# A selective-scan layer behind three banded triangle layers: a third operand ring fed from DRAM, pairs of states multiplied at once, and stores moved behind loads

## The reference

```python
# layers 0, 1, 2, on xn = _ln(_gn(x)) * scale + bias
left = (xn @ Wl + bl) * mask * sigmoid(xn @ Wlg + blg)
right = (xn @ Wr + br) * mask * sigmoid(xn @ Wrg + brg)
out_gate = sigmoid(xn @ Wog + bog)
out = _banded_ingoing(left, right, 4)       # nine taps along one axis, 64 channels
out = _ln(out, out_norm_scale, out_norm_bias) * out_gate
return out @ Wo + bo

# layer 3, on _gn(x), for each of 256 columns over 256 time steps
xi, z = split(xs @ W_in)
xc = silu(causal_conv4(xi) + conv_b)
dt_r, Bc, Cc = split(xc @ W_x)              # 2, 16 and 16 wide
dt = softplus(dt_r @ W_dt + b_dt)           # 64 channels
h = exp(dt * A) * h + dt * B * x            # 64 channels x 16 states, step by step in time
y = einsum('bds,bs->bd', h, C) + xc * D_skip
return (y * silu(z)) @ W_out
```

## Time and profile before

| | |
|---|---|
| median of 3 runs | 2915.89 us (2911.53 to 2921.84) |
| the profiled execution | 2918.08 us, its span 2916.3 us |
| layer 0, 1, 2 of the triangle part | 30 to 404, 404 to 776, 776 to 1208 us |
| scan layer | set up from 1221 us, first scan 1254.4, last scan ends 2901.5 |
| busy over the span | PE 81%, DVE 80%, POOL 70%, ACT 64% |
| granted clock, mean | 0.94 of 2.4 GHz |

### The profile page before, as it was taken

The page is one execution under the profiler, slowest core; times in us unless marked ns, Lnnn a source line. Parts: engine busy times, 40 slices in busy tenths (PEclk is TensorE's granted clock), DMA queues, the critical chain, the costliest instruction groups (busy, mean ns, idle before and its releaser), DMA issues.

```text
span 2916.3 us, 37812 instructions
## 1 busy us (share of the span) xinstructions
PE 2360.2 (81%) x13018; PEld 741.1 (25%) x13018; DVE 2325.2 (80%) x2039; ACT 1853.9 (64%) x2534; POOL 2052.0 (70%) x1194
## 2 busy tenths in 40 slices
PE   4889878898888977478788887888878788787886
PEld 1233122441224421122222222222222222222221
DVE  5655566655565544389999999999999999999997
ACT  3624656245562434377778777777877778777773
POOL 2544244542445422269999999999999999999998
PEclk9999999999998988789999999999999999999997
DMA  4798316983159845676777767767777776767774
GB/s 162 244 328 247 106 45 211 342 275 108 52 183 343 276 136 149 134 178 169 185 176 180 188 166 187 177 175 183 174 188 172 184 178 177 189 165 188 177 176 113
DMA packets 257980, 538.30 MB, mean 185 GB/s; under 512 B 39624, under 2 KB 150992, under 8 KB 256896
## 3 DMA queue, kind: packets, MB, share of 16 engines
q1 hardware_dynamic: 230896, 469.09, 59.2%
q0 software_dynamic: 19040, 64.24, 7.5%
q10 hardware_dynamic: 7856, 2.56, 0.4%
HBM read 396.46 MB, written 139.33 MB: 184 GB/s over the span
## 4 chain that ended last, share of the span: by engine, by line
DVE 24%; issue 16%; ACT 9%; PE 7%; POOL 1%; DMA 0%; ACTq 0%; DVEq 0%; SPq 0%; POOLq 0%
DVE m_hs L473 13%; DVE m_pb L468 12%; ACT m_da L410 4%; PE m_pb L304 2%; ACT L366 1%; ACT m_act L358 1%; ACT L352 1%; PE m_py L284 1%; PE m_misc L242 1%; PE m_py L277 1%; ACT m_act L364 1%; POOL m_hs L486 1%; DMA m_dtb<-dt_rows 0%; PE m_misc L234 0%; PE m_misc L265 0%
## 5 line engine op out<-in xcount | busy, mean ns | idle before, releaser
L486 POOL TENSOR_TENSOR m_hs<-m_hs,m_cs 128x1024 f32<-128x1024 f32 x512 | 1200.4, 2359 | 130.2 <-DVE m_hs L473 80.2
L473 DVE TENSOR_TENSOR_SCAN m_hs<-m_da,m_pb 128x1024 f32<-128x1024 f32 x416 | 951.3, 2287 | 19.1 <-ACT m_da L410 4.7
L304 PE MATMUL m_pb<-m_dtx,late 64*128 64x512 f32 x1664 | 502.3, 677 | 233.7 <-DVE m_hs L473 226.2
L468 DVE TENSOR_TENSOR m_pb<-m_pb,m_bs 128x1024 f32<-128x1024 f32 x416 | 502.8, 1209 | 9.2 <-PE m_pb L304 9.0
L410 ACT ACTIVATE m_da<-m_dtb,m_a_neg 128x1020 f32<-128x1020 f32 x416 | 466.5, 1143 | 3.5 <-DMA m_dtb<-dt_rows 1.3
L1484 POOL TENSOR_TENSOR t_xc<-t_xc,big 128x512 f32<-128x512 f32 x96 | 120.2, 1270 | 333.2 <-DVE big L1390 333.0
L304 PEld LDWEIGHTS m_pb<-m_dtx,late 64*128 64x128 f32 x1664 | 155.3, 200 | 555.6 <-DVE m_hs L473 320.1
L284 PE MATMUL m_py<-m_hs,late 128*32 128x512 f32 x2048 | 277.0, 613 | 7.3 <-POOL m_hs L486 7.3
L1362 DVE SCALAR_TENSOR_TENSOR t_xc<-t_bank,t_vec,t_xc 128x512 f32<-128x512 f32 x96 | 72.0, 750 | 244.2 <-PE t_bank L1052 244.2
L1247 ACT ACTIVATE t_sq<-t_bank 128x512 f32<-128x512 f32 x192 | 106.9, 598 | 227.3 <-PE t_bank L1091 227.1
L1481 POOL TENSOR_TENSOR t_sq<-big 128x512 f32<-128x512 f32 x96 | 102.9, 1082 | 186.2 <-ACT big L1229 109.2
(11 more groups left out here) (160 smaller groups left out, 3847.0 us busy)
## 6 DMA issues: line engine op xcount, KB each, us to landing
m_dtb<-dt_rows SPq DMA_DIRECT2D x512, 512.0 KB, 5.7
late<-right_factor POOLq DMA_DIRECT2D x102, 512.0 KB, 6.2
right_factor<-t_tile SPq DMA_DIRECT2D x192, 256.0 KB, 3.9
t_tile<-band_out SPq DMA_DIRECT2D x183, 256.0 KB, 4.1
band_out<-t_vwin SPq DMA_DIRECT2D x48, 512.0 KB
band_out<-t_vwin SPq DMA_DIRECT2D x48, 480.0 KB
dt_rows<-m_dt SPq DMA_DIRECT2D x64, 256.0 KB, 4.6
t_xc<-in_x_cm SPq DMA_DIRECT2D x4, 2048.0 KB, 14.5
```

The costliest lines, as they stand in the source:

```text
L304: m = nc.tensor.matmul(pb[s % 2][:, half(n)], spread[rows, dg, :], dtx[par][rows, half(q)], start=True, stop=True)
L468: nc.vector.tensor_tensor(products, products, bs[q][:, :], ALU.mult).then_inc(u_done, 1)
L473: nc.vector.tensor_tensor_scan(hs[:, g % H_RING, :], decays, products, 0.0, ALU.mult, ALU.add).then_inc(h_ready, 1)
L486: nc.gpsimd.tensor_tensor(hs[:, g % H_RING, :], hs[:, g % H_RING, :], cs[q][:, :], ALU.mult).then_inc(hc_ready, 1)
```

## The change

Scan layer. `POOL_U` differs by the parity of the chunk: three products in even chunks (steps 5, 10, 15), four in odd ones (4, 8, 12, 15), 16 more in all. dt*x for these products no longer comes by TensorE and ScalarE: SyncE stores both halves of `dtx` to DRAM in step 2 of the same chunk and reads eight rows back, each to 16 partitions, into `ub`, now a ring of three. GpSimd's multiply by C runs in odd steps alone, over two slots of `hs` at once. Triangle layers. bc3 is a step later in the plan and stands near the front of it, behind the gate projection on TensorE and at the front of the part that waits for matmuls on VectorE. SyncE loads unit 14 two steps earlier than it did and unit 15 one step; the gates of unit 0 are opened ahead of its squares.

```diff
-    POOL_U = (5, 10, 15)
-    UB_RING = 2
+    POOL_U = ((5, 10, 15), (4, 8, 12, 15))
+    UB_RING = 3
...
-        USE = {op: i for i, op in enumerate(("u5", "bq1", "cq1", "u10", "x", "z", "dt", "u15", "bq0", "cq0"))}
-        OWN_USE = ("u5", "bq1", "cq1", "u10", "u15")
+        USE = {op: i for i, op in enumerate(("bq1", "cq1", "x", "z", "dt", "bq0", "cq0"))}
+        OWN_USE = ("bq1", "cq1")
...
+        def pool_step(j):
+            kk, i = divmod(j, PER_TWO)
+            par = int(i >= len(POOL_U[0]))
+            return S * (2 * kk + par) + POOL_U[par][i - len(POOL_U[0]) * par]
...
             "gpsimd": {1: [(OWN, "u5")], 3: [(POST, "gate1")], 6: [(OWN, "u10")], 9: [(PRE, "dtx0")], 10: [(PRE, "dtx1")], 11: [(OWN, "u15")],
                        13: [(OWN, "gate0")]},
-            "sync": {14: [(POST, "store")], 15: [(PRE, "dt_rows")]},
-        }
+            "sync": {2: [(OWN, "dtx_rows")], 4: [(OWN, "u5")], 6: [(OWN, "u10")], 8: [(OWN, "u15")], 14: [(POST, "store")], 15: [(PRE, "dt_rows")]},
+        }, {
+            "gpsimd": {1: [(OWN, "u4")], 3: [(POST, "gate1")], 5: [(OWN, "u8")], 8: [(OWN, "u12")], 9: [(PRE, "dtx0")], 10: [(PRE, "dtx1")], 11: [(OWN, "u15")],
+                       13: [(OWN, "gate0")]},
+            "sync": {2: [(OWN, "dtx_rows")], 4: [(OWN, "u4")], 5: [(OWN, "u8")], 7: [(OWN, "u12")], 11: [(OWN, "u15")], 14: [(POST, "store")], 15: [(PRE, "dt_rows")]},
+        })
...
+                    if s % 2 == 0:
+                        return
                     g_.wait_ge(h_ready, g + 1)
-                    nc.gpsimd.tensor_tensor(hs[:, g % H_RING, :], hs[:, g % H_RING, :], cs[q][:, :],
-                                            ALU.mult).then_inc(hc_ready, 1)
+                    two = hs[:, (g - 1) % H_RING:(g - 1) % H_RING + 2, :]
+                    nc.gpsimd.tensor_tensor(two, two, cs[q][:, :].unsqueeze(1).to_broadcast([P, 2, W]), ALU.mult).then_inc(hc_ready, 2)
...
                         j, q = pool_products(k, int(op[1:])), int(op[1:]) // DG
+                        g_.wait_ge(ub_loaded[j % UB_RING], 16 * (j // UB_RING + 1))
                         for n in range(2):
-                            g_.wait_ge(misc_used[n], use(k, op) + 1)
+                            g_.wait_ge(misc_used[n], use(k, f"bq{q}") + 1)
                         nc.gpsimd.tensor_tensor(ub[j % UB_RING][:, :], ub[j % UB_RING][:, :], bs[q][:, :], ALU.mult).then_inc(ub_ready, 1)
                         return
                     q = int(op[3])
                     g_.wait_ge(misc_used[q], use(k, "dt") + 1)
+                    if not early(k, 2):
+                        g_.wait_ge(dtx_stored[par], stores_of(k - 2, par))
                     nc.gpsimd.tensor_tensor(dtx[par][:, half(q)], dt[:, half(q)], act[par][:, half(q)], ALU.mult).then_inc(dtx_ready, 1)
...
+                def load_u(k, par, s):
+                    j = pool_products(k, s)
+                    q, i = divmod(s, DG)
+                    sp.wait_ge(dtx_stored[par], stores_of(k, par))
+                    if j >= UB_RING:
+                        sp.wait_ge(h_ready, pool_step(j - UB_RING) + 1)
+                    rows = dtx_dram[par, q, DG * DGS[i]:DG * DGS[i] + DG, :, :].rearrange("d n c -> d (n c)")
+                    sp.dma_start(ub[j % UB_RING][:, :],
+                                 bass.AP(rows.tensor, rows.offset, [[0, P // DG], [W, DG], [1, W]])
+                                 ).then_inc(ub_loaded[j % UB_RING], 16)
...
+                    if op == "dtx_rows":
+                        sp.wait_ge(dtx_ready, 2 * k + 2)
+                        if not early(k, 2):
+                            sp.wait_ge(ub_ready, pool_products(k - 1, 0))
+                        for n in range(2):
+                            sp.dma_start(dtx_dram[par, :, :, n, :].rearrange("q d c -> d q c"),
+                                         dtx[par][D * n:D * n + D, :].rearrange("d (q c) -> d q c", q=2)).then_inc(dtx_stored[par], 16)
+                        return
...
                 for n in blk[::2]:
-                    steps[at]["bc3"] += [n, n + 1]
+                    steps[at + 1]["bc3"] += [n, n + 1]
                     at += 2 if at < 69 else 1
...
+        LOADS = [[] for _ in STEPS]
+        for n in A3:
+            LOADS[A3_STEP[n] - {14: 3, 15: 2}.get(n, 1)].append(n)
...
-                        for n in STEPS[s + 1]["a3"] if s + 1 < len(STEPS) else ():
+                        for n in LOADS[s]:
                             load_out(l, n)
...
                         for n in st["a3"]:
                             project(l, "og", n, w_og, 4, flip=1)
+                        for n in st["bc3"]:
...
+                        for n in st["a3"]:
                             for p in range(2):
                                 wait_bank(p, (l, "c3", n, p))
...
                             tables(SIGS)
-                            if n >= LATE:
+                            if n == 0 or n >= LATE:
                                 open_gates(l, n)
...
+                        for n in st["bc3"]:
+                            b = bc3_bank(n)
+                            v.wait_ge(full[b], use[l, "bc3", n])
+                            v.wait_ge(free[2], use[l, "y1", n])
+                            nc.vector.tensor_tensor(xn_unit(n), xn_unit(n), bank[b][:, :], ALU.mult).then_inc(free[b], 1)
                         for n in st["y2"]:
```

More of the change, by code:

```diff
@@ L243, in pre @@
                                              start=True, stop=True).then_inc(misc_ready[q], 1)
[L244 to L249, removed]
-                        for n in range(2):
-                            rows = slice(D * n, D * n + D)
-                            nc.tensor.matmul(misc[n][:, :], spread[rows, dg, :], dtx[par][rows, half(q)],
-                                             start=True, stop=True).then_inc(misc_ready[n], 1)
                     elif op == "dt":
@@ L754, in numbering @@
                         fill(7, (l, "lt", k))
+                    for n in st["bc3"]:
+                        fill(bc3_bank(n), (l, "bc3", n))
                     for n in st["a3"]:
@@ L786, in numbering @@
                         fill(band_bank(t), (l, "band", t))
-                    for n in st["bc3"]:
-                        fill(bc3_bank(n), (l, "bc3", n))
                     for b in st["root1"]:
@@ L1083, in _ @@
                             project(l, "og", n, w_og, 4, flip=1)
+                        for n in st["bc3"]:
+                            rows, i = rstd_rows(l, "root3", n)
+                            cg = 64 * (i % 2)
+                            b = bc3_bank(n)
+                            wait_bank(b, (l, "bc3", n))
+                            nc.tensor.matmul(bank[b][:, :], sel3[cg:cg + 64, i // 2, :], rows[cg:cg + 64, :],
+                                             start=True, stop=True).then_inc(full[b], 1)
+                        for n in st["a3"]:
                             for p in range(2):
@@ L1126, in _ @@
                             band(l, t)
-                        for n in st["bc3"]:
-                            rows, i = rstd_rows(l, "root3", n)
-                            cg = 64 * (i % 2)
-                            b = bc3_bank(n)
-                            wait_bank(b, (l, "bc3", n))
-                            nc.tensor.matmul(bank[b][:, :], sel3[cg:cg + 64, i // 2, :], rows[cg:cg + 64, :],
-                                             start=True, stop=True).then_inc(full[b], 1)
             @block.scalar
@@ L1385, in _ @@
                             band(l, t)
-                        for n in st["bc3"]:
-                            b = bc3_bank(n)
-                            v.wait_ge(full[b], use[l, "bc3", n])
-                            v.wait_ge(free[2], use[l, "y1", n])
-                            nc.vector.tensor_tensor(xn_unit(n), xn_unit(n), bank[b][:, :], ALU.mult).then_inc(free[b], 1)
                         for n in (STEPS[s - 1]["bc3"] if s else []) + (st["bc3"] if s == len(STEPS) - 1 else []):
@@ L1608, in __init__, with layers @@
             at += size
-def layers(nc, w, scratch, x3, dt_dram, out):
+def layers(nc, w, scratch, x3, dt_dram, dtx_dram, out):
     with ExitStack() as ctx:
```

58 lines of the change are left out of this document (30 added, 28 removed).

## The result

The changed kernel took 3005.7 us (median of 6 runs, 3000.4 to 3011.8), the kernel before 2917.5 beside it: ratio 1.0304, interval 1.0286 to 1.0322. It is 88 us slower, against a forecast of 70 us faster. The profiled execution has a span of 2998.6 us at a granted clock of 0.891 (before 0.942).

The account below looks back on a forecast made before the run. VectorE was taken to bound the scan layer; in the triangle layers TensorE was busiest, in layer 2 waiting for loads behind SyncE's stores. 2918.1 - 59 (triangle) - 12 (scan) = 2847, stated as 2846 us, range 2830 to 2878.

Parts of the forecast that it names:

- ScalarE loses 96 x 2 copies, TensorE 384 matmuls: both off the path, 0.: Scan layer: work taken from ScalarE and TensorE was claimed to change the time by 0 us.
- Scan sum, 12 us.: Scan layer: 19 us of VectorE products saved, less 4 of waits and 3 at the end, gains 12 us.
- The pair: Scan layer: one GpSimd multiply by C over two slots, 2048 elements, worked out at 4.53 us.
- u4: Scan layer: GpSimd's product of step 4, forecast 0.1 us late for VectorE.
- Rivals 2 and 3: Scan layer: 2, GpSimd products late, no gain, 2859 us, 15%; 3, GpSimd becomes the bound, up to 3220, 4%.
- DMA: Scan layer: 219 GB/s, 90% of a 242 ceiling, cost 0; forecast wrong if ScalarE waits for dtb.
- Rival 4: Scan layer: DMA becomes the bound if the ceiling falls to 200 GB/s, 144 us slower, 3000 us; 3%.
- Layer 2, "43": Third triangle layer: SyncE's next loads ahead of its x stores remove TensorE's waits, gaining 43 us, between 20 and 57.
- the triangle sum: Three triangle layers: 43 + 11 + 5 = 59 us gained, between 25 and 71.
- On TensorE the neighbours are the same, so I cost the move at nothing.: Triangle layers: moving bc3 from a step's end to the next step's front costs TensorE 0 us.
- Unit 14's load 11: Triangle layers: loading unit 14 at step 58, not 60, removes its wait: 3 x 3.7 = 11 us, between 0 and 11.
- unit 0's gates 5: Triangle layers: unit 0's gates ahead of its squares on ScalarE spare TensorE's wait, 3 x 1.8 = 5 us.

Follow-up runs that it names:

- fill_idle: Changed kernel plus 2, 2 and 3 matmuls that nothing reads in TensorE's idle stretches at steps 4, 8 and 12 of odd chunks: 2912.9 us.
- odd_z7: Changed kernel with odd chunks' GpSimd products at steps 5, 9, 13, 15 and z matmuls at step 7, not 6, in both chunks: 2888.0 us.
- tri_stores: Kernel before plus earlier loads of units 14 and 15, unit 0's gates first, SyncE's x stores a step later; bc3 unmoved: 2869.6 us.
- loads_gates: Kernel before with only the loads of units 14 and 15 earlier and unit 0's gates ahead of its squares: 2905.5 us.
- x_out_moved: Changed kernel; in odd chunks convolution matmuls at steps 3 and 4, not 4 and 5, and output matmuls at 10, not 9: 2920.1 us.
- fill: Changed kernel plus TensorE matmuls whose result nothing reads, four passes at steps 0, 3 and 10 of every chunk: 2941.3 us.
- x_moved: Changed kernel; in odd chunks the convolution's matmuls at steps 3 and 4 of TensorE's table, not 4 and 5: 2947.2 us.

## Why the prediction was wrong, by its steps

- **"ScalarE loses 96 x 2 copies, TensorE 384 matmuls: both off the path, 0."** The step that failed: in the scan layer TensorE was put at nothing, and its queue was not walked for the new steps 4, 8 and 12. The missing matmuls are one half of it. With the products at 5, 10 and 15 they are missing too, TensorE's idle stretches grow only from 0.81 to 1.87 and from 0.22 to 1.32 us at their old places, the spread behind each still takes 1.13 us, and the kernel takes 2909.0 us. (The long stretch at step 15, 4.00 us before and 3.4 here, was there all along.) At steps 4, 8 and 12, which have no spread, the stretches are 2.40 to 4.19 us, and what followed ran at 1.2 GHz. fill_idle shows what that costs at these steps: 3005.7 - 2912.9 = 93 us for seven idle-time matmuls in every second chunk.
- **Steps 4, 8 and 12 were costed as 5, 10 and 15.** This is the other half. The prediction walked GpSimd's queue for them and never TensorE's. A GpSimd step s of even number has the sum, in this table at two of three places also the convolution or the output, between spread s+1 and spread s+2: with the convolution 6.2 us of work at 2.4 GHz for 5.8 us of cover. For s odd the sum has run before the release. The same four products on 5, 9, 13 and 15 (with z moved) take 2888.0 us; the price of the placement with its clock is 3005.7 - 2888.0 = 118 us.
- **Scan sum, 12 us.** VectorE's arithmetic was right: with the waits gone, the scan part gains 15 us. Two chunks take 102 us in odd_z7.
- **GpSimd.** The pair takes 4530 ns against 4.53 us worked out. The Trainium skill, GPSIMD Engine Reference, section "Performance versus the Vector engine", gives 4497 ns for a tensor_tensor of 2048 fp32 elements; the trace agrees within 1%. u4 was late by 0.16 us against 0.1, and the waits for ub are 1.6 us in all. Rivals 2 and 3 did not come.
- **DMA.** Share 0.87, 213 GB/s, ub landing in 9.9 us; dtb 6.9 (5.7 in the earlier trace rows), just under the 7 to 9 forecast. ScalarE's wait of 24.8 us met the condition that I had named as making the forecast wrong, but the cause was another: in odd_z7 it waits 92.5 and the kernel is faster. Rival 4 put the ceiling at 200 GB/s; odd_z7 holds 225. The prediction's 219 GB/s counts two stores of dtx in two chunks where there are four (64 in 32 chunks); with them its sum gives 225. The load's lateness did count once, through the z matmuls.
- **Layer 2, "43".** The SyncE argument was right: 36 us by tri_stores against loads_gates, 30 of it seen in layer 2 of the two traces (475.1 and 445.0 us from its first matmul to the first scan). In the changed kernel layer 2 took 36.5 us less by that count, with 17.7 us of waits for loads left where about 10 were forecast. The term was some 7 to 13 us too large. (The upper bound of the triangle sum is 57 + 11 + 5 = 73, not 71.)
- **"On TensorE the neighbours are the same, so I cost the move at nothing."** Wrong, and the second step that failed. The neighbours are the same, but the wait in front of them is not: bc3 had been the cover of the wait for the squares (5.7 us, now 23.1). The wait that the prediction did name, of y2 behind VectorE's multiply, was not covered by 1.09 us of centring either (3.2 us, now 27.2). Together they cost 26 to 34 us by the medians, in layers 0 and 1.
- **Unit 14's load 11, unit 0's gates 5.** Together 12 by loads_gates. In the changed kernel the wait partly moved to unit 12 (its centring starts at 279.11 against 276.78) and unit 14 starts at 298.14, against 298.31 in the kernel before.

By the medians: triangle -59 forecast, -13 measured; scan -12 forecast, +102 measured. Not settled: how the 93 us of clock and the part of the order divide, since either repair alone removes most of the waits (of 115.9 us, fill_idle leaves 30.4 and x_out_moved 33.1). Not run: steps 4, 8 and 12 with dt*x still spread by TensorE, which would separate the missing matmuls from the placement; fill, with unread matmuls at their old steps, brings 64 us back and is the nearest to it.

## What to carry to other kernels

Before work is taken off an engine "with slack", walk that engine's queue from each release to the next need, with each duration at both clock levels: idle time that grows by two microseconds can double what comes behind it (here 2.85 us against 1.14 in x_moved). Work moved within a step may be the cover of a wait; look at what the engine waits for once it is gone. And where a queue's order is the trouble (SyncE's stores ahead of loads), change that order alone.
